# Token tower with a long convolution and a routed feed-forward layer: half of the batches routed inside the gather stage, half inside the expert stage

## What is computed

```
emb   = word_emb[x] + pos_emb                        # 64 x 128 x 192
g_j   = relu(mean over g of (adj_j @ word_emb[ids_j]) @ W_j.T + b_j)   # three graphs, 16 each
h     = layernorm([emb, g_0, g_1, g_2] @ W_proj.T + b_proj) * gamma + beta
k     = implicit filter (128 taps x 192 channels)
h     = h + causal_conv(layernorm(h), k) + layernorm(h) * bias
xn    = layernorm(h);  logits = xn @ Wr.T            # 8 experts
top 2 of 8, softmax over the two
h     = h + sum over the two of weight * (gelu(xn @ Wi[e].T + bi[e]) @ Wo[e].T + bo[e])
```

## Time and profile before

| what | us |
|---|---|
| median of 3 runs (1094.46 to 1096.25) | 1096.01 |
| span of the profiled execution, first to last instruction | 995.9 |
| around the span, median less span | 100.1 |
| gather stage, start to the last landing | 336.9 |
| last landing to the first up matmul of an expert tile | 165.5 |
| first up matmul to the end | 493.5 |

### The profile page before, as it was taken

One profiled execution on the slowest core, in us unless ns is written; L12 is line 12 of the kernel. 1 busy time (PEld: TensorE's weight loads), 2 busy tenths in 40 slices (PEclk: granted clock), 3 DMA queues, 4 the chain that ended last, 5 costly groups with the idle time before them and its releaser, 6 DMA issues.

```text
span 995.9 us, 22850 instructions
## 1 busy us (share of the span) xinstructions
PE 869.3 (87%) x7469; PEld 822.9 (83%) x7469; DVE 656.0 (66%) x2142; ACT 536.0 (54%) x1271; POOL 644.7 (65%) x552
## 2 busy tenths in 40 slices
PE   3959898998898739893889999999999999999993
PEld 2959898998898738892679999999999989898993
DVE  3167857776867565978756776666667656666662
ACT  1222223213312325599667777777777767677761
POOL 6777777777777300100067886777778768788886
PEclk9957556556756669996699999999999999999997
DMA  8437547457465429855946446745744543343454
GB/s 245 131 87 248 179 153 257 136 200 225 157 207 195 126 86 282 225 166 131 245 101 149 61 60 158 191 61 122 199 83 63 130 96 61 59 60 59 61 57 44
DMA packets 99788, 138.31 MB, mean 139 GB/s; under 512 B 13427, under 2 KB 81430, under 8 KB 97654
## 3 DMA queue, kind: packets, MB, share of 16 engines
q0 software_dynamic: 39552, 53.26, 28.1%
q1 hardware_dynamic: 59142, 73.59, 24.3%
q10 hardware_dynamic: 1008, 10.34, 2.8%
HBM read 98.14 MB, written 39.02 MB: 138 GB/s over the span
## 4 chain that ended last, share of the span: by engine, by line
PE 29%; DMA 22%; POOL 22%; issue 12%; DVE 8%; ACT 4%; DVEq 2%; SPq 1%; POOLq 0%; ACTq 0%
DMA out<-Hs,id_s 20%; POOL ev_g L521 13%; POOL emb_g L512 5%; PE bank L799 3%; PE bank L801 3%; PE bank L800 3%; POOL blob L537 3%; PE bank L780 2%; PE bank L781 2%; PE bank L784 2%; PE bank L783 2%; PE bank L782 2%; DVE hstats L1157 2%; ACT adj_s L956 1%; PE bank L763 1%
## 5 line engine op out<-in xcount | busy, mean ns | idle before, releaser
L975 ACT ACTIVATE Hs<-bank,U 128x256 bf16<-128x256 f32 x426 | 214.0, 502 | 126.0 <-PE bank L784 126.0
L551 POOL DMA_INDIRECT out<-Hs,id_s x142 | 233.5, 1645 | 65.6 <-issue 45.6
L537 POOL DMA_INDIRECT blob<-xtab_d,id_g x142 | 151.6, 1068 | 122.7 <-DVEq L1340 79.6
L521 POOL DMA_INDIRECT ev_g<-in_word_emb,ids_i x192 | 189.7, 988 | 58.5 <-issue 57.9
L976 ACT ACTIVATE Hs<-bank,U 128x256 f32<-128x256 f32 x426 | 216.4, 508 | 0.0
L799 PE MATMUL bank<-U,Hs 128*128 128x192 bf16 x852 | 210.0, 246 | 0.3 <-issue 0.3
L801 PE MATMUL bank<-U,Hs 128*128 128x192 bf16 x852 | 208.8, 245 | 0.0
L800 PE MATMUL bank<-U,Hs 128*128 128x192 bf16 x852 | 208.5, 245 | 0.0
L1362 DVE TENSOR_TENSOR Hs<-Hs 128x512 bf16<-128x512 f32 x213 | 146.8, 691 | 92.1 <-ACT Hs L976 92.0
L780 PE MATMUL bank<-wst,U 128*128 128x256 bf16 x426 | 116.6, 274 | 1.3 <-DVE wst L1351 1.3
L781 PE MATMUL bank<-wst,U 128*128 128x256 bf16 x426 | 116.7, 274 | 0.0
(11 more groups left out here) (216 smaller groups left out, 1643.2 us busy)
## 6 DMA issues: line engine op xcount, KB each, us to landing
adj_s<-in_adj SPq DMA_DIRECT2D x48, 256.0 KB, 7.3
ev_g<-kpad_d SPq DMA_DIRECT2D x24, 512.0 KB, 5.8
U<-blob_d SPq DMA_DIRECT2D x14, 771.0 KB, 5.0
wst<-in_wsrc SPq DMA_DIRECT2D x8, 1344.0 KB
blob_d<-blob ACTq DMA_DIRECT2D x7, 1443.0 KB
U<-blob_d SPq DMA_DIRECT2D x14, 672.0 KB, 5.7
xtab_d<-U SPq DMA_DIRECT2D x4, 1552.0 KB, 17.0
out<-Hs SPq DMA_DIRECT2D x4, 1536.0 KB, 12.8
```

Source lines behind the costliest of these rows:

```text
L521: pool.indirect_dma_start(ev_g[:, p, j, b, :], None, t["word_emb"], bass.IndirectOffsetOnAxis(ap=ids_i[:, 1 + j, i * Q + b:i * Q + b + 1], ...
L537: pool.indirect_dma_start(xg_f[:, q % RX, h, :], None, xtab_d, bass.IndirectOffsetOnAxis(ap=id_g[:, 2 * q + h:2 * q + h + 1], axis=0)).the ...
L551: pool.indirect_dma_start(out, bass.IndirectOffsetOnAxis(ap=id_s[:, 2 * q + h:2 * q + h + 1], axis=0), yo[:, q % RY, h, :], None, compute_ ...
L975: f(hh[w][:, d, :], ps, ACT.Gelu, bias=bi[:, d:d + 1])
```

## The change

The batches are split into halves of 32 (8 groups each).

- Half 0: convolution and routing are cut into small steps (`route(0)`, a generator on each engine). From group 8 on, tables named `beside` say how many steps each engine takes at four places in a group. What is left runs after the last group.
- Half 1: the same steps (`route(1)`) are taken inside the expert tiles 0 to 22, by tables named `pieces`. Tiles 0 to 24 hold picks of half 0 alone; picks of half 0 that don't fit in full tiles go with half 1 into tiles 25 to 70. Before tile 25 GpSimd waits for half 1's rows and indices.
- Convolution: the 32 batches of a channel are now the weights (128 x 32) and the reversed Toeplitz matrix (128 x 128) streams, four channels in four groups of 32 columns of the array; ScalarE copies the 512 columns out, TensorE transposes them back in four pieces, VectorE adds. 12 chunks of 16 channels per half. ScalarE no longer reverses a unit, but issues most Toeplitz loads itself, two per chunk. Each half loads all 24 units.
- Graph vectors: the column mean (32 columns wide, one of use) is the weight and the gathered rows stream, 192 columns, four batches in four column groups. ScalarE copies 576 columns out, and six more matmuls (`graph_columns`) pick the vectors out of it.
- Expert preparation: one expert per group in groups 0 to 7 in two sets of rooms, stored by SyncE.
- Buffers: hidden buffers 3 to 2, output buffers 4 to 3, projection banks 4 to 2, Toeplitz ring 4 to 6. The 85 idle matmuls go.
- The loops over groups and tiles are written out.

```diff
+            def graph_vectors(i, p, j):
...
+                for b in range(Q):
+                    k = j * Q + b
+                    mm(bank[3][32 * b:32 * b + 32, j * D:j * D + n], cs[:, p, k:k + 32], ev_g[:, p, j, b, 0:n], start=True, stop=True)
...
+            def graph_columns(i, p):
+                pe.wait_ge(gsum_ready, i + 1)
+                for j in range(GRAPHS):
+                    for c, first in ((0, 0), (1, D - 128)):
+                        last = mm(bank[3][:, 16 * c + j * Q:16 * c + (j + 1) * Q], gsum[p][:, j * D + first:j * D + first + 128], pick_b[:, :],
+                                  start=True, stop=True)
+                last.then_inc(gpick, 1)
...
+                def products(c):
+                    after(pe, conv_copied[x], c)
+                    for u in (2 * c, 2 * c + 1):
+                        pe.wait_ge(toep_in[x][u % RING], 16 * (u // RING + 1))
+                    for at in range(2 * CC):
+                        u = 2 * c + at // CC
+                        last = mm(bank[conv_bank][32 * (at % 4):32 * (at % 4) + 32, at // 4 * 128:at // 4 * 128 + 128],
+                                  Ut[x][:, 2 * CC * c + at, :], reverse(toep[x][u % RING][:, at % CC, :]), start=True, stop=True)
+                    last.then_inc(conv_out[x], 1)
...
+            beside = {8: (0, 0, 0, 1), 9: (1, 1, 1, 1), 10: (1, 1, 1, 1), 11: (1, 1, 1, 1), 12: (1, 1, 1, 2),
+                      13: (1, 1, 1, 2), 14: (1, 1, 1, 2), 15: (1, 1, 0, 1)}
...
+                if q == TA - 1:
+                    rows_stored(1)
...
+                limit = TA if q < TA - 1 else NT
+                while fetched < min(limit, q + FIRST + 1 + min(q // 2, AHEAD - FIRST)):
...
+                def copied(c):
+                    act.wait_ge(conv_out[x], c + 1)
+                    after(act, conv[x], c - 1)
+                    f(turned_s[x][c % 2], bank[conv_bank][:, :], ACT.Copy).then_inc(conv_copied[x], 1)
+                    for u in range(2 * c + RING, min(2 * c + RING + 2, UNITS)):
+                        load_toep(act, x, u)
...
+                for g in range(TG):
+                    scaled(g)
+                    if g % 4 == 1:
+                        row_parts(4 + g // 4)
+                    yield
```

The tables of the expert stage, on TensorE (places: after the up matmuls, between the halves of the down matmuls, after them):

```diff
+                if q <= 6:
+                    return 1, 0, 1
+                if 7 <= q <= 11:
+                    return 1, 1, 1
+                if q in (12, 14, 15):
+                    return 1, 0, 0
+                if q == 16:
+                    return 0, 0, 1
+                return (1, 1, 1) if 17 <= q <= 21 else (0, 0, 0)
```

More of the change, by code:

```diff
@@ L657, in _ @@
-            column_means(0, 0)
-            steps(pe, NQ // 2, pair, last=1)
-            pe.wait_ge(rows_done, NQ)
-            def chunk(it, s):
-                c = it * RING + s
-                pe.wait_ge(turned, c + 1)
-                for k in range(CC):
-                    n = 2 if k < CC - 1 else 1
-                    last = mm(bank[6 + s % 2][:, k * B:(k + n) * B], tp[:, s % 2, k, :],
-                              Ut[:, bass.ds(c * CC + k, n), :].rearrange("p c b -> p (c b)"), start=True, stop=True)
-                last.then_inc(conv, 1)
@@ L696, in score @@
-            def score(i):
-                p = i % 2
-                g = next(k for k, (first, n) in enumerate(GROUPS) if i * Q < first + n)
-                pe.wait_ge(xnT_ready, i + 1)
-                after(pe, chosen, g - 1)
-                for h in range(Q // 2):
-                    at_h = (i * Q - GROUPS[g][0] + 2 * h) * E
-                    for r in range(XR):
-                        last = mm(bank[3 + g % 2][:, at_h:at_h + 128], xnT[:, p, XR * h + r, :], wr[:, r, :], start=r == 0, stop=r == XR - 1)
-                last.then_inc(logits, 1)
@@ L982, in _ @@
                 after(act, down, q - W3 + 1)
-                hidden(q, q % W3)
+                advance(late_route, n[0])
+                for c in range(0, FC, 2):
+                    hidden(q, c)
+                advance(late_route, n[1])
+                if q + 3 == TA:
+                    for _ in late_route:
+                        pass
+                    f(junk[:, :], mean_w[:, 0:1], ACT.Gelu)
         @block.vector
@@ new lines, in _ @@
+            early = route(0)
+            beside = {8: (0, 0, 1, 1), 9: (1, 1, 1, 2), 10: (1, 1, 1, 2), 11: (1, 1, 0, 2), 12: (1, 0, 0, 2),
+                      13: (1, 0, 0, 2), 14: (2, 0, 1, 2), 15: (2, 1, 1, 0)}
+            row_sums(0, 0)
+            row_sums(1, 1)
+            filter_argument(0)
+            for i in range(NQ):
+                p = i % 2
+                n = beside.get(i, (0, 0, 0, 0))
+                if 1 <= i <= E:
+                    split_lo(i - 1)
+                if i + 2 < NQ:
+                    row_sums(i + 2, p)
+                advance(early, n[0])
+                rows(i, p, n)
+                if i == 0:
@@ L1133, in pairs @@
                     filter_argument(1)
                     filter_taps()
-                if not (isinstance(it, int) and it > 0):
-                    split_lo(it)
-                if not (isinstance(it, int) and it == NQ // 2 - 1):
-                    row_sums(2 * it + 3, 1, it + 2)
-                rows(2 * it + 1, 1)
-            steps(dve, NQ // 2, pairs, last=1)
-            split_lo(E - 1)
-            fence()
-            v.memset(seg[:, :, :], 1.0)
-            fence()
-            v.memset(seg[:, :, 0:1], 0.0)
```

1215 lines of the change are left out of this document (666 added, 549 removed).

## The result

The kernel after takes 1176.4 us (median of 4 runs, 1169.7 to 1183.6), the kernel before 1095.2 beside it: a ratio of 1.081 (95% interval 1.068 to 1.094). The forecast was 1085 us, with a range up to 1122: **slower by 81 us, not faster by 11**.

The account below looks back on a forecast made before the run. GpSimd bounds the gather stage, TensorE and GpSimd the expert tiles, with an unbounded gap between. Front -78, half 1 in tiles +54, ScalarE +8, hand-over +5 sum to -11: 1085 us from 1096.0, range 1052 to 1122.

Parts of the forecast that it names:

- 1062 with the front at 90: Full-overlap rival, chance 0.27: column groups fully side by side, no waits, 1062 us; with the front saving 90, 1052.
- The 100.1 us around the span are held fixed: Whole kernel: the time outside the recorded 995.9 us span was taken as unchanged and added to the new span.
- TensorE gains at least 3 us per group ... I take no delay: Gather stage: cheaper graph vectors make room on TensorE for route steps of about 6 us in groups 9 to 15; no delay.
- From the last gather to the first up matmul: Front: half 0's routing beside the gathers brings the first up matmul from 502.4 to 424.5 us, -78.
- Convolution in tiles: Half 1 in expert tiles: 12 chunks at 2.23 us, 26.8 us; products 1.8 each, between 0.93 side by side and 3.7 serial.
- Pairs: Half 1 in expert tiles: 16 pairs of transposes, a plain matmul and logits on TensorE, 0.55 and 0.67 us each, 19.5 us.
- Choices, rounds and rows in tiles 12 to 23: Half 1's later steps: TensorE one-hot rounds 7.2 us, ranks and counts 0.8, ScalarE's excess +8.
- VectorE's share ... hides: Half 1 in tiles: VectorE's added 65 us over 22 tiles, 3 per tile beside 4.5, is hidden under 8.8 us tiles.
- ScalarE +8: Tiles 16 to 21: scalings and row writes make ScalarE 9.3 us per tile against TensorE's 6.6 + 1.3, costing 8 us.
- the rival of program order: Expert tiles: steps wait for other engines, 1 us in each of 23 tiles plus fewer hidden buffers, 1110 us; chance 0.20.
- Hand-over at tile 25: After tile 24 GpSimd issues five tiles' fetches, 13 us, before tile 22's stores, with fewer output buffers: +5 us.
- The rival on the slower side, column groups not side by side: Convolution products run serially, 3.7 us a chunk, +23 in tiles and +20 beside gathers: 1128 us; chance 0.13.

Follow-up runs that it names:

- b0: Kernel before, unchanged, run and profiled again: 1083.9 us, its profiled execution with a span of 1092.8 us.
- a_gv: Kernel after with the full-array graph vectors of the kernel before, convolution still in column groups: 1159.1 us.
- b_gv: Kernel before with the graph vectors alone put in four column groups: 1114.7 us.
- a_gvfew: Kernel after with the graph vectors of before, and half 0's convolution chunks 2 to 11 cut to a quarter of products and transposes: 1145.4 us.
- a_pace: Kernel after with a memset and a drain on GpSimd after each gather, gathers 3.45 us apart: 1651.8 us.
- b_p1: Kernel before with one short memset, without a drain, on GpSimd after each gather: 1086.2 us, ratio 1.002.
- b_p2: Kernel before with two short memsets, without a drain, on GpSimd after each gather: 1081.4 us, ratio 1.002.
- b_pace: Kernel before with a memset and a drain on GpSimd after each gather, gathers 3.45 us apart: 1609.8 us.

## Why the prediction was wrong, point by point

The sum was made against the recorded span: 985 + 100. The span came out 191.8 us longer than 985. By the table: first up matmul at 577.2 instead of 424.5 (+152.7), tiles 0 to 24 (+32.8), the rest (+6.3). 97 of these are in b0 already (1092.8 against 995.9). Two sums of the prediction are a little off and decide nothing: 16 gathers at 0.99 + 0.30 us are 20.7 us, not 20.1, and 1062 with the front at 90 is 1050, not 1052.

- **"The 100.1 us around the span are held fixed": failed, and with it the reading of the gather stage.** A profile whose span is 100 us short of the runs of its kernel misses a piece of each run; it is not a constant around it. In b0 it sits where the change puts its work.
- **"TensorE gains at least 3 us per group ... I take no delay": the step that cost most.** The last gather is 57 us later than in b0: 25 for the graph vectors in column groups (a_gv; 28 by b_gv), 20 for the products of 7.5 chunks (a_gvfew), 11 left. The gain in TensorE's own time is real (busy 74 of 135 us, 93 in b0) and worth nothing beside gathers 1.25 us apart: the hand-overs to ScalarE and back, two in a group where there was one, wait for a signal that comes 8 to 13 us late in groups 1 to 8. The wait that the prediction put at nothing is the one that decides. With gathers at 1.45 us the same kernel has its last gather at 417.6.
- **From the last gather to the first up matmul: right in mechanism, 26 us short here.** 89.3 forecast (167.3 less 78), 115.3 measured, 80.6 where the gathers leave time (a_pace). TensorE is a group behind: the last graph vectors start at 490.2, 28 us after the last gather, and VectorE's last rows wait for them.
- **Convolution in tiles: over-priced.** The products take 1.1 us a chunk, not 1.8. Tiles 2 and 3, with two chunks each and no waits, take 9.8 us where 6.6 is the rule, so 1.6 us a chunk with its transposes, not 2.23. Tiles 0 to 5 are 19 us longer than in b0, not 27 (28 longer than in the recorded profile, whose tiles 0 to 5 are 9.5 us shorter than b0's). The ends of the bound, 0.93 and 3.7, were measured almost exactly (1.1 and 3.7). By the Trainium skill, "TensorEngine Tiling (Array Packing)", Theoretical Speedup, weights of at most 32 columns run up to four times as fast; by that the trace agrees, with a factor of 3.4 (3.68 / 1.08).
- **Pairs: 1.5 us each, not 1.22.** Tiles 6 to 11 are 24 to 26 us longer against 19.5. Tiles of three pairs take 11.1 us, 6.6 + 4.5, TensorE nearly full.
- **Choices, rounds and rows in tiles 12 to 23: 16 forecast, 36 measured**, and 35 to 38 in every variant that left this part and the convolution of half 1 alone. "VectorE's share ... hides" and "ScalarE +8" looked at each engine alone. This is the rival of program order, in half of the tiles instead of all; whether the hidden buffers that it names are the reason was not tried.
- **Hand-over at tile 25: +13.5, not +5.** The ten fetches do stand ahead of the stores, from 827.5 to 840.6 us, as the prediction says. What it left out is that the pipeline runs dry: VectorE waits 9.3 us once at L1475, where it needs a free output buffer, and tile 25 takes 17.4 us, at a granted clock of 0.71. The smaller rings of hidden and output buffers cost nothing visible behind it: tiles 26 to 70 take 323.2 us against 325.5.
- The rival on the slower side, column groups not side by side, had the right sign and a wrong mechanism. That in the runs GpSimd waits for TensorE in the gather stage was in no rival; the recorded profile did not show it.

## What to carry to other kernels

Set the span of a profile beside the times of the runs before using one row of it; if they differ by more than a few us, the profile shows another execution, and a sum made on it has no base. Work put "beside" a stage that is bound by another engine is free only while every signal in its chain is on time, so ask who waits for its hand-overs, not only how busy the engines are. Count the hand-overs of a rewritten step as well as its matmuls. Where GpSimd issues long series of indirect transfers, try them a tenth of a microsecond further apart: here that alone made the kernel before about 1% faster and the kernel after 4%.

## What the runs showed that was not expected

- With gathers of 128 rows issued every 1.25 us, TensorE, VectorE and ScalarE are held up in steps of 0.7 us from 11 to 16 us into the series, but not in every execution: VectorE's step in 6 groups of b0 and of after, 5 of b_p1, 3 of b_p2, none of a_gv and of the recorded profile. At 1.38 and 1.45 us it is held up in 1 of 80 groups (five runs), at 3.45 us in none of 48.
- Late signals from TensorE remain at 1.38 us; at 1.45 us they are mostly gone, at 3.45 us none is left in b_pace and a_pace.
- That the pace matters is shown in the kernel after: its last gather moves from 461.9 to 422.0 and 417.6 us, and with memsets that leave the pace alone only to 458.5. In the kernel before the last gather (397.0, 407.8) moves no more than between executions at one pace (392.0 to 405.1). What is behind the hold-ups is open, and so is why the recorded execution had the same pace of 1.25 us and none at all.
- With a drain on GpSimd behind a gather and its memset, 2.3 to 2.4 us pass before the next gather; one or two memsets without a drain (0.08 us each) add some 0.01 us, since they fall into the 0.30 us between two gathers.
- 16 float32 products of 128 by 128 with 32 columns: 1.1 us in four column groups, 3.7 on the full array at 2.4 GHz, and 7.0 there at 1.2 GHz.
